# Three woven streams in place of two in a fused attention, feed-forward, recurrence and expert kernel

## What is computed

```python
# layer 0, attention: 16 heads of 16, window of 128; 4 latent heads on 64 pooled tokens
q, k, v = split(x @ qkv_w + qkv_b)
local = softmax(q k / 4 over the last 128 positions) @ v
remote = softmax(rq rk / 4 over earlier chunks of 8) @ rv @ rout_w + rout_b
gate = sigmoid(local @ gl_w + remote @ gr_w)
y = (gate * local + (1 - gate) * remote) @ out_w + out_b
# layer 0, feed-forward: ternary weights, 1024 wide
y = gelu(x @ ternary(W1).T + b1) @ ternary(W2).T + b2
# layer 1, attention: a recurrence over the tokens, 16 heads, state 16 x 16
o_t = r_t (s + exp(u + k_t) v_t);  s = exp(w_t) s + k_t v_t
y = (layernorm_per_head(o) * r) @ W_o.T
# layer 1, feed-forward: 16 experts, top 4, and a shared one
y = sum_e comb[:, e] * (silu_and_mul(x @ w13[e].T) @ w2[e].T) + shared(x)
```

## Time and profile before

| | us |
|---|---|
| profiled execution | 2294.64 |
| its span, first to last instruction | 2292.8 |
| median of three executions | 2293.34 |
| TensorE matmuls busy | 1842.8 (80%) |
| VectorE busy | 1607.1 (70%) |
| ScalarE busy | 852.3 (37%) |
| POOL busy | 701.2 (31%) |
| mean granted TensorE clock | 0.886 |

### The profile page before, as it was taken

The page is one execution under the profiler, slowest core; times in us unless marked ns, Lnnn a source line. Parts: engine busy times, 40 slices in busy tenths (PEclk is TensorE's granted clock), DMA queues, the critical chain, the costliest instruction groups (busy, mean ns, idle before and its releaser), DMA issues. The chain is left out here.

```text
span 2292.8 us, 32504 instructions
## 1 busy us (share of the span) xinstructions
PE 1842.8 (80%) x10626; PEld 1163.0 (51%) x10626; DVE 1607.1 (70%) x3353; ACT 852.3 (37%) x1804; POOL 701.2 (31%) x619
## 2 busy tenths in 40 slices
PE   0887998899799889979987997898666652499978
PEld 0454454455445445544544554454434442499963
DVE  3224589669758866976896697689669965477745
ACT  0242443345334333524442353334322222366632
POOL 0000033114103311420330141033018873466641
PEclk9777989899999998989999998989886666699989
DMA  4000000000000000000000000000103234576666
GB/s 136 0 1 10 0 1 1 20 1 1 10 11 1 1 20 1 1 10 11 1 1 20 1 1 10 11 1 1 32 15 109 100 111 141 198 247 187 182 215 267
DMA packets 83763, 119.77 MB, mean 52 GB/s; under 512 B 12729, under 2 KB 70397, under 8 KB 83456
## 3 DMA queue, kind: packets, MB, share of 16 engines
q1 hardware_dynamic: 69376, 80.59, 11.5%
q0 software_dynamic: 13056, 35.68, 4.2%
q10 hardware_dynamic: 1152, 1.18, 0.1%
HBM read 67.71 MB, written 51.79 MB: 52 GB/s over the span
## 5 line engine op out<-in xcount | busy, mean ns | idle before, releaser
L653 DVE TENSOR_TENSOR_SCAN s_buf<-r_work,kvb 128x512 f32<-128x512 f32 x256 | 352.8, 1380 | 0.0
L838 POOL TENSOR_TENSOR p_buf<-s_buf,r_work 128x512 f32<-128x512 f32 x128 | 152.9, 1195 | 458.4 <-DVE s_buf L653 451.0
L911 ACT ACTIVATE probs<-bank_s,nmx 128x256 f32<-128x256 f32 (+1 forms) x512 | 186.6, 450 | 110.3 <-DVE nmx L516 109.3
L838 POOL TENSOR_TENSOR r_work<-s_buf,r_work 128x512 f32<-128x512 f32 x128 | 158.4, 1239 | 191.7 <-DVE s_buf L653 191.4
L803 POOL TENSOR_TENSOR rstd<-vare,mhalf 128x4 f32<-128x4 f32 x48 | 48.4, 1008 | 509.9 <-DVE vare L449 509.9
L929 ACT ACTIVATE pt<-bank_s 128x1024 f32<-128x1024 f32 (+1 forms) x128 | 117.4, 918 | 216.7 <-PE bank_s L1219 216.7
L642 DVE TENSOR_TENSOR kvb<-r_work,bank 128x512 f32<-128x512 f32 x256 | 174.5, 682 | 21.6 <-PE bank L1337 13.3
L516 DVE TENSOR_REDUCE nmx<-bank_s 128x4 f32<-128x1024 f32 (+1 forms) x128 | 137.5, 1074 | 48.0 <-PE bank_s L1169 47.7
L1896 POOL DMA_INDIRECT y_rows<-w_in_ys,m_y_idx x144 | 141.7, 984 | 89.7 <-ACT w_in_ys L1982 53.8
L1061 PE MATMUL bank_s<-wmask,ident_b 128*128 128x512 bf16 x356 | 109.6, 465 | 44.4 <-DVE vare L449 28.5
L1336 PE MATMUL bank<-v_hi,sel_v 128*128 128x512 f32 x256 | 132.1, 516 | 14.8 <-DVE kvb L642 8.1
(11 more groups left out here) (403 smaller groups left out, 4204.8 us busy)
## 6 DMA issues: line engine op xcount, KB each, us to landing
m_xs<-x_rows SPq DMA_DIRECT2D x146, 144.0 KB
w_lo<-y_rows SPq DMA_DIRECT2D x4, 2048.0 KB, 21.9
w_hi<-y_rows SPq DMA_DIRECT2D x4, 2048.0 KB, 23.3
w_in_ys<-in_w SPq DMA_DIRECT2D x17, 256.0 KB, 3.9
x_new<-in_x SPq DMA_DIRECT2D x8, 512.0 KB, 3.7
x_after_rwkv<-x_b SPq DMA_DIRECT2D x8, 512.0 KB, 3.8
m_x_all<-x_after_rwkv SPq DMA_DIRECT2D x8, 512.0 KB, 4.1
out<-m_x_all SPq DMA_DIRECT2D x8, 512.0 KB, 3.0
```

The source lines that it names most:

```text
L653: V.tensor_tensor_scan(s_buf[:, n % 2, 1:S + 1], dec[:, n // HD, :], kvb[:, n % 2, :], 0.0, ALU.mult, ALU.add).then_inc(sem["state"], 1)
L838: G.tensor_tensor(p_slot(n), s_buf[:, n % 2, 0:S], rf[:, n // HD, :], ALU.mult).then_inc(sem["rs"], 1)
L911: ins = A(probs[:, n % 2, x, h * w:h * w + w], score_banks[n % 2][:, x, h * w:h * w + w], ACT.Exp, bias=nmx[:, n, 2 * x + h:2 * x + h + 1])
```

## The change

Stream a now holds attention alone (38 steps). The feed-forward is a stream f of its own, one batch behind, and the recurrence is split at scan 20: in pass b, stream r holds scans 20 to 33 and the tail of batch b-2, then head and scans 0 to 19 of batch b-1. The order strings are new. Batch 0's attention runs alone; the pass of b = 1 has attention 1, feed-forward 0 and the first part of recurrence 0; the loop covers b = 2 to 7; the end stage has feed-forward 7, the rest of recurrence 6, all of recurrence 7 and the expert rows.

The feed-forward uses two banks. Sixteen units (8 blocks times 2 halves of 256 tokens) go one by one through half of A0, and both halves of the output accumulate in A1. Its work tiles lie in pt and probs, which the local attention uses too, so scores(0) of a batch waits for a_final of the batch before. Attention has A2, A3, A4 and waits more often for an eviction before it writes a bank again. x is loaded into a new tile x_next, and ScalarE copies it to x_new. Of the dummy matmuls, 37 of 91 per pass stay (norm1 5, gate 18, recurrence 14).

The core of the diff:

```diff
+FS = S // 2
+N_UNITS = 2 * NF
+SPLIT = 20
+OWN_A, OWN_F = 25, 5
...
-STEPS_A = (["norm1", "turn1", "q", "k", "v", "lat_scores", "lat_turn0", "lat_turn1", "lat_out", "lat_nt", "remote", "scores0"]
-           + LOCAL_STEPS + ["gate", "mix", "out", "resid1", "norm2", "turn2"]
-           + [f"ffn{f}" for f in range(NF + 2)] + ["ffn_y", "ffn_tok", "resid2"])
-STEPS_HEAD = (["rnorm", "rturn", "rmix0", "rmix1", "rmix2", "rmix3", "rproj0", "rproj1", "rproj2", "rproj3", "rbonus", "rspread"]
-              + [f"scan{n}" for n in range(N_SCAN + 2)])
+STEPS_T = (["norm1", "turn1", "q", "k", "v", "lat_scores", "lat_turn0", "lat_turn1", "lat_out", "lat_nt", "remote", "scores0"]
+           + LOCAL_STEPS + ["gate", "mix", "out", "resid1"])
+STEPS_F = ["norm2", "turn2"] + [f"ffn{n}" for n in range(N_UNITS + 2)] + ["ffn_y", "ffn_tok", "resid2"]
+STEPS_HEAD = ["rnorm", "rturn", "rmix0", "rmix1", "rmix2", "rmix3", "rproj0", "rproj1", "rproj2", "rproj3", "rbonus", "rspread"]
+STEPS_SCAN = [f"scan{n}" for n in range(N_SCAN + 2)]
+STEPS_TAIL = ["o_tok", "o_var", "wait0", "wait1", "wait2", "wait3", "wait4", "wait5", "o_norm", "o_back", "o_out", "rresid"]
...
-    tensor="aaarrarrrrrrararrarrraararraararrarrarararrraararararrraarrarararrraararaaraaarrrrrraarrrrraaaaarraaaaraaraaaaa",
+    tensor="rafarafafrfafrfrffrffrffrrfrfrffrarfrfrfrrraafraffrrrrararaaararrrrarrraraarrarrrararrarararrarrarraararrafaraarararara",
...
-def batches_woven(eng, order, order_end, attention_ffn, rwkv_head, rwkv_tail, expert_rows):
-
-    weave(order, [(STEPS_A, attention_ffn(0))], [])
-    with eng.Fori(1, B) as b:
-        weave(order, [(STEPS_A, attention_ffn(b))], [(STEPS_HEAD, rwkv_head(b - 1)), (STEPS_TAIL, rwkv_tail(b - 1))])
-    weave(order_end, [(STEPS_ROWS, expert_rows())], [(STEPS_HEAD, rwkv_head(B - 1)), (STEPS_TAIL, rwkv_tail(B - 1))])
+    assert not any(steps.values())
+
+
+def batches_woven(eng, order, order_end, attention, ffn, head, scans, tail, expert_rows):
+
+    def rest(b):
+        return [(STEPS_SCAN[SPLIT:], scans(b, SPLIT, N_SCAN + 2)), (STEPS_TAIL, tail(b))]
+
+    def first(b):
+        return [(STEPS_HEAD, head(b)), (STEPS_SCAN[:SPLIT], scans(b, 0, SPLIT))]
+
+    weave(order, a=[(STEPS_T, attention(0))])
+    weave(order, a=[(STEPS_T, attention(1))], f=[(STEPS_F, ffn(0))], r=first(0))
+    with eng.Fori(2, B) as b:
+        weave(order, a=[(STEPS_T, attention(b))], f=[(STEPS_F, ffn(b - 1))], r=rest(b - 2) + first(b - 1))
+    weave(order_end, f=[(STEPS_F, ffn(B - 1))], r=rest(B - 2) + first(B - 1) + rest(B - 1), e=[(STEPS_ROWS, expert_rows())])
...
+        x_next = sb("x_next", [P, NT, D])
         x_new = sb("x_new", [P, NT, D])
...
-        o_raw = sb("o_raw", [P, S])
...
+        o_raw = work[:, 8, :]
+        blockones = probs[:, 0, 0, 0:P]
+
+
+        f_xn, f_out, f_raw = pt[:, 0], pt[:, 1], probs[:, :, 0, 0:FS]
...
-                sp.wait_ge(sem["x_free"], at(b, "x_free", 1))
-                sp.dma_start(x_new[:], rows(t["x"][bass.ds(b + 1, 1)])).then_inc(sem["x_in"], 16)
+                sp.wait_ge(sem["pooled"], at(b, "pooled", 1))
+                sp.wait_ge(sem["x_taken"], at(b, "x_taken", 1))
+                sp.dma_start(x_next[:], rows(t["x"][bass.ds(b + 1, 1)])).then_inc(sem["x_in"], 16)
 
             def store(b):
                 sp.wait_ge(sem["x_final"], at(b, "x_final", 1))
                 sp.dma_start(rows(x3[bass.ds(b, 1)]), x_b[:]).then_inc(x_stored, 16)
 
-            sp.dma_start(x_new[:], rows(t["x"][0:1])).then_inc(sem["x_in"], 16)
-            next_x(0)
-            with sp.Fori(1, B - 1) as b:
+            sp.dma_start(x_next[:], rows(t["x"][0:1])).then_inc(sem["x_in"], 16)
+            for b in range(2):
                 next_x(b)
-                store(b - 1)
-            store(B - 2)
+            with sp.Fori(2, B - 1) as b:
+                next_x(b)
+                store(b - 2)
+            store(B - 3)
...
+                sc.wait_ge(sem["x_in"], at(b, "x_in", 16))
+                if not (isinstance(b, int) and b == 0):
+                    sc.wait_ge(sem["x_free"], at(b, "x_free", 0))
+                A(x_new[:], x_next[:], ACT.Copy).then_inc(sem["x_taken"], 1)
...
+                def keep(half):
+                    sc.wait_ge(sem["f_y"], at(b, "f_y", NF * half + NF))
+                    for k in range(NK):
+                        A(f_out[:, k, half * FS:half * FS + FS], A1[:, k * FS:k * FS + FS], ACT.Identity, bias=b2[:, k:k + 1]).then_inc(sem["fy_sb"], 1)
+
                 yield "norm2"
                 for k, src in enumerate((A0, A1)):
-                    sc.wait_ge(sem["turned"], at(b, "turned", 2 + k + 1))
-                    A(hiT[:, k, :], src[:], ACT.Copy).then_inc(sem["evened"], 1)
+                    sc.wait_ge(sem["f_turned"], at(b, "f_turned", k + 1))
+                    A(hiT[:, k, :], src[:], ACT.Copy).then_inc(sem["f_evened"], 1)
                 yield "turn2"
-                for f in range(NF + 2):
-                    if f < NF:
-                        sc.wait_ge(sem["h_ps"], at(b, "h_ps", f + 1))
-                        if f >= 2:
-                            sc.wait_ge(sem["g_lo"], at(b, "g_lo", f - 1))
-                        g_ins = A(work[:, f % 2, :], bank[f % 3][:], ACT.Gelu, bias=b1[:, f:f + 1])
-                        g_ins.then_inc(act_own, 1)
-                        if f >= 2:
-                            sc.wait_ge(sem["f_y"], at(b, "f_y", f - 1))
-                        sc.wait_ge(act_own, b * NF + f + 1)
-                        A(g_hi[:, f % 2, :], work[:, f % 2, :], ACT.Copy).then_inc(sem["g_hi"], 1)
-                    yield f"ffn{f}"
-                sc.wait_ge(sem["f_y"], at(b, "f_y", NF))
-                for k, src in enumerate((A3, A4)):
-                    A(work[:, 2 + k, :], src[:], ACT.Identity, bias=b2[:, k:k + 1]).then_inc(sem["fy_sb"], 1)
+                for n in range(N_UNITS + 2):
+                    f = n % NF
+                    if n == NF + 2:
+                        keep(0)
+                    if n < N_UNITS:
+                        sc.wait_ge(sem["h_ps"], at(b, "h_ps", n + 1))
+                        if n >= 2:
+                            sc.wait_ge(sem["g_lo"], at(b, "g_lo", n - 1))
+                        A(f_raw[:, n % 2, :], A0[:, 0:FS], ACT.Gelu, bias=b1[:, f:f + 1]).then_inc(sem["g_raw"], 1)
+                        if n >= 2:
+                            sc.wait_ge(sem["f_y"], at(b, "f_y", n - 1))
+                        sc.wait_ge(sem["g_raw"], at(b, "g_raw", n + 1))
+                        A(g_hi[:, n % 2, 0:FS], f_raw[:, n % 2, :], ACT.Copy).then_inc(sem["g_hi"], 1)
...
-                if not (isinstance(b, int) and b == 0):
-                    pe.wait_ge(sem["var"], at(b, "var", 0))
-                    repeat(A3, 4)
-                    pe.wait_ge(sem["rstd"], at(b, "rstd", 0))
-                    repeat(A3, 8)
...
                 yield "remote"
+                if not (isinstance(b, int) and b == 0):
+                    pe.wait_ge(sem["a_final"], at(b, "a_final", 0))
                 scores(0)
...
-                yield "norm2"
-                pe.wait_ge(sem["var"], at(b, "var", 2))
-                repeat(A4, 4)
-                pe.wait_ge(sem["rstd"], at(b, "rstd", 2))
-                repeat(A4, 8)
-                pe.wait_ge(sem["x_free"], at(b, "x_free", 1))
-                repeat(A4, 8)
-                pe.wait_ge(sem["var"], at(b, "var", 3))
-                repeat(A4, 4)
-                pe.wait_ge(sem["rstd"], at(b, "rstd", 3))
-                repeat(A4, 1)
-                turn(b, "normed", 1, "turned", (A0, A1), xn)
-                yield "turn2"
-
-                def up(f):
-                    if f >= 3:
-                        pe.wait_ge(sem["g_hi"], at(b, "g_hi", f - 2))
+
+            def ffn(b):
+
+                def up(n):
+                    t, f = divmod(n, NF)
+                    if n:
+                        pe.wait_ge(sem["g_raw"], at(b, "g_raw", n))
                     for k in range(NK):
                         for c, part in enumerate((hiT, loT)):
-                            ins = T.matmul(bank[f % 3][:], w1t[:, k, f * P:(f + 1) * P], part[:, k, :],
+                            ins = T.matmul(A0[:, 0:FS], w1t[:, k, f * P:(f + 1) * P], part[:, k, t * FS:t * FS + FS],
                                            start=k == 0 and c == 0, stop=k == NK - 1 and c == 1)
                     ins.then_inc(sem["h_ps"], 1)
 
-                def down(f):
-                    pe.wait_ge(sem["g_lo"], at(b, "g_lo", f + 1))
-                    for k, dst in enumerate((A3, A4)):
-                        for c, part in enumerate((g_hi[:, f % 2, :], g_lo[:, f % 2, :])):
-                            ins = T.matmul(dst[:], w2t[:, f, k * P:(k + 1) * P], part, start=f == 0 and c == 0,
-                                           stop=f == NF - 1 and c == 1)
+                def down(n):
+                    f = n % NF
```

(27 more changed lines are left out.)

280 lines of the change are left out of this document (143 added, 137 removed).

## The result

The changed kernel takes 2316.7 us (median of 4, 2314.9 to 2320.0) against 2294.1 for the kernel before on the same chip: ratio 1.0105, 95% interval 1.0087 to 1.0123, about 1% slower. Forecast were 2175 us, and 2085 to 2260 as range. The profiled execution has a span of 2313.5 us.

A forecast was written before the change was run, and what follows sets the result against it. No engine is full over a pass: holes beside serial chains were to be filled, TensorE's 171 us the tighter bound. 58 + 155 + 160 + 6 x 185 + 298 + 393 = 2174, given as 2175 us; range 2085 to 2260.

The forecast's parts named there:

- middle and end of a pass: From scores0 to resid1: 103 us becomes 108, with VectorE busy 92 and TensorE 99.
- sixteen g_lo: VectorE in a pass: sixteen of 256 replace eight of 512, 6.8 us against 5.5, +1.2.
- the 54 dummies: TensorE's dummy matmuls at norm1, norm2 and around the feed-forward: removal takes 15 us off its busy time.
- The halved matmuls: TensorE in the feed-forward: 128 of 256 columns at 0.19 us replace 64 of 512, 24 us, +9.5.
- TensorE's sum: Busy time in a pass: 177 - 15 + 9.5 = 171 us, the tighter lower bound of a pass.
- The new wait of ScalarE's copy for the store: In the middle, x_b of batch b-1 waits for batch b-2's store: 0 to 4 us, 2 taken.
- The b = 1 pass: First woven pass, no rest of an older recurrence: 160 us, bounds 140 and 201.
- T: Length of a new loop pass: 185 us, 16 less than 201; equal time needs 205, parts outside cost 1065.8.
- A: Rival: feed-forward units of 3.3 us set the front, 89 us; T = 197, total 2248; chance 0.18.
- B: Rival: weave fills better, TensorE 164 us, front 67, middle 103; T = 170, total 2085; chance 0.20.
- C: Rival: without dummies TensorE's clock falls to 0.70 in the passes; T = 225, total 2415; chance 0.09.
- D: Rival: static engine orders block each other; T = 203 to 205, nothing changes, total 2290; chance 0.03.

The follow-up runs named there:

- a_half: Changed kernel with each of the head's eight projections as one matmul rather than two, half the sum left out: 2291.7 us, ratio 0.9996 to the kernel before.
- a_kv: Changed kernel with VectorE's products ahead of the scans over 256 of 512 columns, half left out: 2303.7 us, ratio 1.0064 to the kernel before.
- a_head: Changed kernel reordered, 4 rather than 7 local tiles among the head's steps, the other tile steps between scans: 2395.1 us, ratio 1.0445 to the kernel before.
- a_more: Changed kernel with 9 rather than 7 local tiles among the head's steps, fewer among the scans behind: 2405.6 us, ratio 1.0502 to the kernel before.
- a_sp16: Changed kernel with 16 rather than 20 of a batch's scans in the pass of its head: 2395.6 us, ratio 1.0452 to the kernel before.
- a_sp24: Changed kernel with 24 rather than 20 of a batch's scans in the pass of its head: 2382.7 us, ratio 1.0395 to the kernel before.
- b_nodum: Kernel before without the 54 dummy matmuls that the change takes out: 2333.5 us, ratio 1.0167 to the kernel before.
- a_fill: Changed kernel with dummy matmuls put back into TensorE's longest holes: 2303.8 us, ratio 1.0053 to the kernel before.
- a_best: Changed kernel with a_fill's dummies and GpSimd's two large attention operations held back by added waits: 2295.4 us, ratio 1.0018 to the kernel before.
- b_half: Kernel before with each of the head's eight projections as one matmul rather than two, half the sum left out: 2241.9 us, ratio 0.9773.
- b_kv: Kernel before with VectorE's products ahead of the scans over 256 of 512 columns, half left out: 2271.3 us, ratio 0.9910.

## Why the prediction was wrong

**The step that failed** is the length of "middle and end of a pass": "TensorE had 17 us of idle in this stretch; I let 8 of the 13 added us go into it and 5 lengthen it: 108." It added up the work of a stretch as if any of it could fill any hole. But 12 of the 17 us lay behind the last scan, beside the end of the attention, in a window of the pass of the earlier trace rows:

```profile
581.70:612.00 30.30, 18.41 (x94) 9.50 (x95) 25.00 (x56) 3.11 (x6) 6.51 (x4) 0.89 0.01 2
```

The added 13 us are the head, and no scan of a batch can run before its head is done, so they came in ahead of all 20 scans and could fill nothing behind them. TensorE's idle time did not fall from 17 us to 9 but grew to 28: 4.0 in the head, 12.1 beside the 20 scans and 12.0 in the stop. The stretch became two: one in which TensorE is the full engine (48.1 of 55.4 us) and one in which VectorE is (67.9 of 73.0). The sum of the slowest engine of each is 116.0, against 99.8 for TensorE over both; that is 16 of the 20 us missed, and the rest is 12.4 us of idle against the 9 allowed. The ledger is arithmetic on the trace. The runs bear on it in part: 7 us less of TensorE's work shorten the head by 3.1 (a_half), 8.6 us less of VectorE's products leave the 20 scans 96% full of VectorE, part of that waiting (a_kv), and tiles and scans can't be traded between the stretches (a_head, a_more, a_sp16, a_sp24), though with orders made by hand. That no better order exists isn't shown.

**Two terms within it were mis-sized.** VectorE has 163.7 us a pass, not 156 to 157: sixteen g_lo take 9.1 us where 6.8 were forecast (0.40 to 0.43 us alone, up to 1.51 beside GpSimd), and other operations are lengthened beside GpSimd as well (without GpSimd's two operations it is busy for 4 us less and the pass is 3 us shorter). And taking out the 54 dummies, which the forecast lets cost nothing, costs 38 us in the old order (b_nodum); putting some back gives 12 us in the new one (a_fill). Mended together they give 4 of the 19 us by which the mean pass missed 185 (a_best: 200.1 for 204.1). What it would take to recover the other 15 is open.

**The other steps.** The halved matmuls were taken at 0.19 us, from the loads of 188 ns; they start 0.12 us apart:

```profile
1238.98 0.28 PE L1289 MATMUL bank_s<-hiT,w1t 128*128 128x256 f32 x1
1239.10 0.29 PE L1289 MATMUL bank_s<-loT,w1t 128*128 128x256 f32 x1
1239.22 0.28 PE L1289 MATMUL bank_s<-hiT,w1t 128*128 128x256 f32 x1
```

so 128 take about 15 us and cost nothing over 64 full ones. The page that the prediction set aside (the Trainium skill, TensorE: Matmul & The Clock Gate, on the back-to-back issue gap and on LDWEIGHTS) is near on the spacing, 109 ns for 0.12 us, though not on the load, 107 ns for 188. TensorE's sum still came out, 169.0 for 171, by two errors against each other: the halves cost nothing instead of 9.5 us, and taking the dummies out took 9.2 us off its busy time rather than 15 (b_nodum, 168.3 us a pass on the mean for 177.5), as more of the rest ran at the lower clock (0.94 on the mean before, 0.88 then). ScalarE has 86.9 us (87). The new wait of ScalarE's copy for the store, 0 to 4 us, was 0 in all six passes of the loop. The b = 1 pass missed (192 for 160) by the same stretch: 273 to 399 us there holds head, 20 scans and tiles, 126 us. "A b = 1 pass off 160 by over 15" was named as a sign of error, and came. It also moved the break-even: the prediction has it at T = 205, but the stages outside T make 1091 us rather than 1065.8, so T would have had to be 200.5. Of the signs of being right, the clock held (0.91 over the six passes, the prediction wanted 0.9; all six of before have 0.94, the 0.96 of the earlier trace rows is one pass), the shares did not: VectorE is busy for 80% of them, not 84, and TensorE for 83%, not over 90.

**The rivals.** A (the feed-forward sets the front) is wrong: the front is 76 us. B is wrong. C has the right direction and a small part of the size: the clock did fall, from 0.94 to 0.91, not to 0.70. D, given 0.03, named T = 203 to 205, which is what came, but as engines that block each other; what came is mostly two stretches with unlike bounds. No rival had a time above before except C, which was given 0.09. Missing was a rival by the recurrence's own chain: head, scans and tail follow each other through the whole pass before (55.6 + 89.4 + 58.5 = 203.5 us), so T could fall only as far as this chain did. That the three add up to the pass follows from how they are cut; that they lie on the path is shown for the head (b_half, 6.9 us a pass for 7 us of work) and in part for the scans (b_kv).

## What to carry to other kernels

Before adding up busy times, follow each serial chain through one whole pass and ask whether it leaves a hole; if it fills the pass, a new weave helps only by what it takes from between the links. Before work is put into idle time, look where in the stretch that idle time lies. Add up the slowest engine stretch by stretch, with stretches cut where a chain forbids work to cross. Give a price to taking dummy matmuls out, and to operations of VectorE on SBUF beside GpSimd. Read every pass of a trace before calling a change of clock an effect.

## What the runs showed of the hardware

**VectorE and GpSimd exclude each other for some operands.** The tiny `rinv` (128x16) takes 0.17 us alone and 0.99 when it meets a product of GpSimd; the scan ahead of it starts beside an earlier product. The lines are VectorE's, then GpSimd's:

```profile
1181.34 1.73 DVE L676 TENSOR_TENSOR_SCAN s_buf<-r_work,kvb 128x512 f32<-128x512 f32 x1
1182.99 0.26 DVE L540 RECIPROCAL rinv<-bank 128x16 f32<-128x16 f32 x1
1183.28 0.99 DVE L541 TENSOR_TENSOR rinv<-rinv,row_loc 128x16 f32<-128x16 f32 x1
...
1186.02 3.25 DVE L567 TENSOR_TENSOR work<-work 128x1024 f32<-128x1024 f32 x1
```
```profile
1180.71 1.28 POOL L863 TENSOR_TENSOR r_work<-s_buf,r_work 128x512 f32<-128x512 f32 x1 [1.16 <-DVE s_buf L676]
1183.15 1.09 POOL L863 TENSOR_TENSOR r_work<-s_buf,r_work 128x512 f32<-128x512 f32 x1 [1.16 <-DVE s_buf L676]
1184.80 3.38 POOL L835 TENSOR_TENSOR work<-work 128x1024 f32<-128x1024 f32 x1 [0.57 <-DVE work L542]
```
